# One-hots of a routing table in wide 16-bit VectorE operations, with a reordered drain of the routers

## The reference, cut to what matters

```
x = x + attention(layernorm(x), ctx, W_k, b_k, gamma, beta)      # x: 4 batches x 512 tokens x 512
x = x + moe(layernorm(x), Wg, W1, W2, W3)

def moe(x, Wg, W1, W2, W3):                                      # 8 experts, hidden size 352
    scores = einsum('btd,ed->bte', x, Wg)
    topk_s, topk_i = top_k(scores, 2)
    w = weights of the two chosen experts: softmax(topk_s), zero elsewhere
    for e in range(8):
        h = silu(x @ W1[e].T) * (x @ W2[e].T)
        y = y + w[..., e:e+1] * (h @ W3[e].T)
```

## Time and profile before

| | |
|---|---|
| time, median of 3 runs | 421.27 us (421.18 to 422.28) |
| time of the profiled execution | 422.17 us |
| its span in the profile | 420.1 us |
| TensorE busy | 366.2 us (87%) |
| VectorE busy | 273.6 us (65%) |
| ScalarE busy | 265.2 us (63%) |
| GpSimd busy | 187.0 us (45%) |
| mean granted TensorE clock | 0.907 of full speed |

### The profile page before, as it was taken

How to read it: one execution, slowest core, us unless ns; L and a number is a source line. 1 busy time by engine, 2 the same in 40 slices (tenths; PEclk the granted TensorE clock), 3 DMA queues, 4 the chain that set the end, 5 groups by cost and what they waited for, 6 DMA issues and landing times.

```text
span 420.1 us, 8336 instructions
## 1 busy us (share of the span) xinstructions
PE 366.2 (87%) x2321; PEld 244.9 (58%) x2321; DVE 273.6 (65%) x724; ACT 265.2 (63%) x457; POOL 187.0 (45%) x221
## 2 busy tenths in 40 slices
PE   6876997996948447799999999999999999999982
PEld 5543665765848234455566666666666666666650
DVE  0252565958668739999776676676676676676670
ACT  2287587855657619789666666666666666666660
POOL 2115364476896661355434434434434434434322
PEclk9998699599555569999999999999999999999997
DMA  7997889964741021224354354354354355354333
GB/s 233 418 420 275 273 290 370 355 230 160 243 166 37 26 75 28 50 52 70 83 103 75 78 102 77 75 103 75 78 102 78 75 102 80 75 100 79 77 48 51
DMA packets 21835, 57.62 MB, mean 137 GB/s; under 512 B 4832, under 2 KB 4960, under 8 KB 20256
## 3 DMA queue, kind: packets, MB, share of 16 engines
q0 software_dynamic: 8736, 20.53, 27.5%
q1 hardware_dynamic: 11040, 21.62, 14.6%
q10 hardware_dynamic: 2016, 14.94, 9.9%
HBM read 38.17 MB, written 18.91 MB: 136 GB/s over the span
## 4 chain that ended last, share of the span: by engine, by line
PE 52%; POOL 7%; DVE 7%; issue 6%; DMA 2%; ACT 2%; ACTq 1%; POOLq 1%; DVEq 0%
PE bank L1220 29%; PE bank L1254 15%; PE bank L1211 3%; POOL stage L429 3%; PE bank L1240 3%; DVE Wp L804 2%; DVE stage L951 1%; DMA out<-kvj_s,sidx 1%; POOL ng_s L469 1%; PE bank L1124 1%; POOL w3rs L476 1%; ACT stage L638 1%; DVE x_s L983 1%; POOL rstd L412 1%; DVE stage L767 1%
## 5 line engine op out<-in xcount | busy, mean ns | idle before, releaser
L951 DVE SCALAR_TENSOR_TENSOR stage<-W,w3sc,stage 128x512 f16<-128x512 f16 x117 | 84.2, 748 | 6.8 <-ACT stage L638 6.8
L1254 PE MATMUL bank<-stage,n_s 128*128 128x512 f16 (+1 forms) x351 | 82.2, 379 | 2.8 <-issue 1.5
L1220 PE MATMUL bank<-Wp,kvg_s 128*128 x480 | 79.9, 317 | 4.6 <-DVE kvg_s L957 4.6
L638 ACT ACTIVATE stage<-W,w3sc 128x512 f16 x117 | 80.2, 718 | 0.0
L1220 PE MATMUL bank<-Wp,kv_s 128*128 x456 | 74.3, 313 | 3.4 <-DVE kv_s L957 3.4
L484 POOL DMA_INDIRECT out<-oT_s,sidx x20 | 34.1, 1704 | 75.1 <-ACT oT_s L665 67.7
L1220 PEld LDWEIGHTS bank<-Wp,kvg_s 128*128 128x128 f16 x480 | 47.3, 99 | 31.5 <-issue 6.1
L484 POOL DMA_INDIRECT out<-kvj_s,sidx x19 | 32.4, 1706 | 66.2 <-ACT kvj_s L665 63.5
L1220 PEld LDWEIGHTS bank<-Wp,kv_s 128*128 128x128 f16 x456 | 44.4, 98 | 28.3 <-issue 4.8
L975 DVE TENSOR_TENSOR n_s<-bank,n_s 128x384 f16<-128x384 f32 x39 | 21.7, 557 | 54.9 <-ACT n_s L651 54.9
L1254 PEld LDWEIGHTS bank<-stage,n_s 128*128 128x128 f16 (+1 forms) x351 | 34.2, 98 | 36.1 <-issue 3.3
(11 more groups left out here) (184 smaller groups left out, 555.2 us busy)
## 6 DMA issues: line engine op xcount, KB each, us to landing
Wp<-in_w ACTq DMA_DIRECT2D x6, 1408.0 KB, 8.7
W<-in_w ACTq DMA_DIRECT2D x8, 768.0 KB, 5.3
stage<-in_xT SPq DMA_DIRECT2D x4, 1024.0 KB, 7.8
W<-in_x SPq DMA_DIRECT2D x12, 256.0 KB, 7.4
out<-W SPq DMA_DIRECT2D x12, 256.0 KB, 5.5
Wp<-in_w SPq DMA_DIRECT2D x2, 1408.0 KB, 12.9
n_table<-n_s SPq DMA_DIRECT2D x8, 256.0 KB, 3.2
n_table<-x_s SPq DMA_DIRECT2D x8, 256.0 KB, 3.0
```

Source lines behind the costliest of these rows:

```text
L638: eng.activation(w3p[t % 2][:, c * D:(c + 1) * D], W3[:, bass.ds(e * W3N + c * D, D)], ACT.Copy, scale=w3sc[:, bass.ds(e, 1)]).then_inc(s_ ...
L951: eng.scalar_tensor_tensor(w3p[r][:, W3N + c * D:W3N + (c + 1) * D], W3[:, bass.ds(e * W3N + c * D, D)], w3sc[:, bass.ds(e, 1)], w3p[r][:, ...
L1220: mm = eng.matmul(bank[2 * which + r][:, 0:H], n_, w_, start=(c == 0 and k == 0), stop=(c == DC - 1 and k == 2))
L1254: mm = eng.matmul(ybank(t - 1)[:, :], h_, w_, start=(c == 0 and k == 0), stop=(c == HC - 1 and k == 2))
```

## The change

The two one-hot matrices of a whole lot are made on VectorE by three instructions, all of whose operands are fp16: row one-hots, column one-hots, and a multiplication of the row one-hots by the token's number. For this, two tables are made once at the start: `steps8` (0 to 127, each number eight times) and `tok16`. The one-hots of a lot now lie interleaved, pair by pair innermost, so TensorE reads each with a step of eight elements. GpSimd makes no one-hots. TensorE's drain is reordered and has no `warm` matmuls. Lot 3 is placed ahead of the last group's router scores on VectorE. The zeros for the dump row are made in slot 17 and stored ahead of the last router weights. The split of expert 1's W1 and W2 on ScalarE goes behind the first `mT_evac`, and VectorE's first low half goes behind the list of experts.

```diff
-WARM_GATHER = 16
-WARM_DRAIN = 8
+WARM_GATHER = 12
...
-        qf = sb("qf", [P, G * TOPK])
-        rf = sb("rf", [P, G * TOPK])
+        qf = sb("qf", [P, G * TOPK], F16)
+        rf = sb("rf", [P, G * TOPK], F16)
+        steps8 = sb("steps8", [P, P, TPB * TOPK], F16)
+        tok16 = sb("tok16", [P, G, TOPK], F16)
...
@@ sync: the dump row's store
             batches(slot)
-            router_store(B - 1)
-
             eng.wait_ge(s_zr, 1)
             eng.dma_start(out[T:T + P, :], zrow[:, :]).then_inc(s_zst, 16)
+            router_store(B - 1)
...
@@ gpsimd: slot
-                if n in (11, 12):
-                    columns(0, 2 * n - 22, 2 * n - 20)
-                if n in (14, 15):
-                    columns(1, 2 * n - 28, 2 * n - 26)
-                if n == 18:
-                    columns(2, 0, 4)
+                if n == 17:
+                    eng.wait_ge(s_mp, B)
+                    eng.memset(zrow[:, :], 0.0).then_inc(s_zr, 1)
             gamma_keys(0)
             batches(slot)
-            columns(3, 0, 3)
-            columns(4, 0, 1)
-
-            eng.wait_ge(s_mp, B)
-            eng.memset(zrow[:, :], 0.0).then_inc(s_zr, 1)
...
@@ scalar: behind the slots
-            w12_high(1, 0)
             router_exp(B - 1)
-            w3_square(4)
-            w12_high(1, 1)
-            for k in range(5, E):
+            for k in range(4, E):
                 w3_square(k)
...
             mT_evac(0)
+            w12_high(1, 0)
+            w12_high(1, 1)
...
@@ vector
-            def columns(q, a, z):
-
-                g0 = GROUPS[q][0]
+            def columns(q):
+
+                g0, m = GROUPS[q]
+                i0, a = g0 % TPB * TOPK, g0 // TPB % 2
+                ring_free(eng, q)
+                cols, ring = slice(g0 * TOPK, (g0 + m) * TOPK), slice(i0, i0 + m * TOPK)
+                shape = [P, P, m * TOPK]
                 eng.wait_ge(s_rqf, 2 * q + 1)
-                ring_free(eng, q)
-                for c in range((g0 + a) * TOPK, (g0 + z) * TOPK):
-                    g, s = c // TOPK, c % RING
-                    eng.tensor_scalar(oh_r[:, s, :], iota[:, :], rf[:, c:c + 1], tok1[:, g:g + 1], ALU.is_equal, ALU.mult).then_inc(s_ohr, 1)
+                eng.tensor_tensor(oh_r[:, a, :, ring], steps8[:, :, ring], rf[:, None, cols].to_broadcast(shape), ALU.is_equal).then_inc(s_ohp, 1)
+                eng.wait_ge(s_rqf, 2 * q + 2)
+                eng.tensor_tensor(oh_c[:, a, :, ring], steps8[:, :, ring], qf[:, None, cols].to_broadcast(shape), ALU.is_equal).then_inc(s_ohc, 1)
+                eng.wait_ge(s_ohp, q + 1)
+                eng.tensor_tensor(oh_r[:, a, :, ring], oh_r[:, a, :, ring],
+                                  tok16[:, g0:g0 + m, :].rearrange("p g k -> p (g k)")[:, None, :].to_broadcast(shape), ALU.mult).then_inc(s_ohr, 1)
...
+                if n == 20:
+                    places(3)
+                    columns(3)
                 b3, i3 = lag(b, i, 4)
...
-                if i == 0 and real(b - 2):
+                if i == 0 and 1 < b < B:
                     places(b - 2)
-                if n in (11, 12):
-                    columns(0, 2 * n - 22, 2 * n - 20)
-                if n in (14, 15):
-                    columns(1, 2 * n - 28, 2 * n - 26)
                 if n == 18:
-                    columns(2, 0, 4)
-                    w12_low(0, 0)
+                    places(2)
+                if n in (11, 14, 18):
+                    columns((n - 11) // 3 if n < 18 else 2)
...
@@ tensor: drain
                 if n == 17:
                     router(B - 1, 0)
-                    rank(2)
                     turn_n(B - 1, 2)
                     router(B - 1, 1)
                 if n == 18:
+                    rank(2)
                     router(B - 1, 2)
-                    warm(ones16[:, :], WARM_DRAIN)
                     turn_n(B - 1, 3)
                 if n == 19:
-                    warm(ones16[:, :], WARM_DRAIN)
+                    table(1)
+                    rank(3)
                     router(B - 1, 3)
-                    table(2)
-                    rank(3)
                 if n == 20:
+                    table(2)
                     rank(4)
                     counts()
                     table(3)
```

More of the change, by code:

```diff
@@ L299, in ring_free @@
         def ring_free(eng, q):
+            eng.wait_ge(s_eoff, 3)
             eng.wait_ge(s_op, B)
@@ L903, in _ @@
             router_weights(B - 1)
-            places(last - 1)
             places(last)
-            columns(last - 1, 0, 3)
-            columns(last, 0, 1)
+            columns(last)
             eng.wait_ge(s_cntp, 1)
@@ L990, in _ @@
             eng.wait_ge(s_et, 1)
+            w12_low(0, 0)
             w12_low(0, 1)
@@ L1181, in slot @@
                     table(0)
-                if n == 16:
-                    table(1)
             eng.wait_ge(s_const, NCONST)
```

33 lines of the change are left out of this document (15 added, 18 removed).

## The result

The changed kernel takes 405.38 us (median of 4 runs, 404.62 to 407.42) against 421.54 us of the kernel before in the same job (421.18 to 422.28). The ratio is 0.9622, with a 95% interval of 0.9584 to 0.966: 16.2 us faster. I had forecast 410.0 us with a range of 406.5 to 416.2. The direction was right; the gain is 4.8 us larger than the sum, and the time lies outside the range. Two later jobs, each with one of the two kernels unchanged, gave 0.9618 and 1.0002 (experiments c2 and c1), so the gap is no accident of one job.

A forecast was written before the change was run, and what follows sets the result against it. Before the tiles, a chain of waits on GpSimd's column one-hots and the dump row's store was taken as the bound. Terms -7.2 + 0 - 3.1 - 1.1 + 0 = -11.4 us gave 410.0 us, range 406.5 to 416.2.

The forecast's parts named there:

- Step A: Slots 11 to 17, to the last normalised group, without GpSimd's column one-hots: -7.2 us.
- the term for the start of slot 11: In slot 11 VectorE has 1.9 us in place of 1.10, and 0.33 us of idle takes some: +0.5 us.
- Step B: From the last normalised group to the last places: again 11.8 us, so a change of 0.
- What is saved pays for columns 2 and 3: In the drain, dropping 16 warm matmuls and L804's 1.68 us offsets the column one-hots of two lots: 0.
- Step C: From the last places to `gidx`: 3.2 us in place of 6.3, as the table no longer awaits GpSimd: -3.1 us.
- rival 1: Wide instructions run at one element per cycle: +6.4 us, some 0.5 of it hidden, 416 us; chance 0.15.
- Rival 3: Wide instructions are slower than one element per cycle, over 1.6 us each; 426 us at the strided price; chance 0.04.
- Step D: From `gidx` to the first gather: 1.1 us in place of 2.24, no longer awaiting the dump row's store: -1.1 us.
- Step E: Start of the tiles: ScalarE's two w12_high fit into its wait for TensorE: 0.
- So it fits, with 0.6 us to spare: 0.: At the start of the tiles, ScalarE's added work takes 4.4 us where its next instruction started 5.0 us later.
- Rival 2: TensorE stays at 2.4 GHz through the drain: 408.3 us, 407 if the walk is pessimistic too; chance 0.11.
- 11 to 12 us from there to `w3rs` as before: Sign expected in the profile after: the time from the first gather to `w3rs` stays unchanged.

The follow-up runs named there:

- c2: The changed kernel timed once more with no edit: 404.72 us, 0.9618 of the kernel before.
- c1: The kernel before timed once more with no edit: 421.42 us, ratio 1.0002; its profiled execution took 421.50 us.
- e4: The changed kernel with the two constant tables `steps8` and `tok16` in fp32 instead of fp16: 411.76 us, 0.9791 of the kernel before.
- e5: The changed kernel with TensorE's old drain and the old places of lots 2 and 3 on VectorE: 407.52 us, 0.9679 of the kernel before.
- e7: The changed kernel with the splits of W1 and W2 of experts 0 and 1 back in their old places: 407.25 us, 0.9686 of the kernel before.
- e3: The kernel before with only the wide one-hots on VectorE; drain, zero store and splits as before: 408.88 us, 0.9687 of the kernel before.
- e1: The kernel before with only the dump row's zeros made in slot 17 and stored ahead of the last router weights: 417.54 us, 0.9907.
- e6: The changed kernel with one low half of expert 0's split put right behind the list of rows, beside the first gather: 407.11 us, 0.9672.
- e8: The changed kernel with 24 more warm matmuls in slots 15 and 16 and 12 more in slot 17: 404.79 us, 0.9617 of the kernel before.

## Why the prediction was wrong

The forecast beside two profiles, c1 for before (421.50 us) and the first of the changed kernel (405.16 us), both of executions near their medians. Each step is the time between the same two instructions in both (c1, then changed):

```
step                                       forecast   measured
A  up to the product of slot 11             +0.5      -0.6   (89.01 -> 88.37)
A  product to last xneg                     -6.0      -6.2   (30.80 -> 24.65)
A  xneg to last normalised group            -1.7      -1.7   (5.11 -> 3.44)
B  to the last places                        0        -0.8   (11.83 -> 11.06)
C  to gidx                                  -3.1      -3.0   (6.29 -> 3.28)
D  gidx to first gather                     -1.1      -1.7   (2.22 -> 0.51)
E  gather to the first copy (kvg_s)          0        -1.3   (6.27 -> 4.94)
E  copy to L629                              0        -0.4   (5.63 -> 5.28)
   the tiles, to the end                     0        -0.5   (262.24 -> 261.77)
sum                                        -11.4     -16.1
```

- *Step A* was right where it was worked out: the slots from the product of slot 11 to `xneg` and the normalisation behind it came within 0.2 us. What failed is the term for the start of slot 11. It took the 0.33 us of idle in the earlier trace rows for the room that slot has; c1 shows 2.47 us in the same code, and in e4, with 1.2 us an instruction, the product is no later (87.83). So no profile shows the 0.5 us. The other 0.6 us of this row are an earlier start of slot 11 than in c1, which is within the spread of profiles (87.02 to 90.72 us) and not shown to come from the change. The base itself was a late execution of that slot, with the last normalised group at 126.00 against 124.92 in c1.
- *Step B* was a walk that came out at no change; it was 0.8 us shorter. e5 and e7 show that both halves of the change matter there: with the old order it is 11.93 us, with the split back in slot 18 of the new order it is 12.56. With the old order the split cost nothing (11.92 in e3), so the 1.68 us counted as saved were not there as a term of their own. "What is saved pays for columns 2 and 3" was nearly right, with 0.8 us over.
- *Step C* was right: 3.28 us against 3.2. The wide instructions of the last pair, the count and the table's copy follow as walked. The price, on which rivals 1 and 3 hung, was right too (0.695 us against 0.69), and e4 shows rival 1's cost about as I had priced it (+6.4 forecast with 0.5 hidden; 7.1 to 7.3 by the medians, 4.9 in the profile). Rival 3 needs over 1.6 us an instruction; nothing of it is there.
- *Step D*: the store as a releaser went, as forecast, but I allowed 0.9 us from `gidx` to the gather, read from the landing of a store to the gather, and 0.2 for `gidx`; all of it takes 0.51 us from `gidx`'s start. The gain was put 0.6 us too low.
- *Step E is the step that failed*: "So it fits, with 0.6 us to spare: 0." It looked at ScalarE alone, and found rightly that its two high halves cost nothing (0.45 us to spare). It put at nothing what GpSimd pays beside VectorE there. In the kernel before, a split with two SBUF inputs started 0.25 us ahead of the first gather and another 0.17 us ahead of `w3rs`, and each held GpSimd up by 1.3 to 1.4 us:

```profile
146.11 1.69 DVE L804 SCALAR_TENSOR_TENSOR Wp<-Wp,wscale 128x1408 f16<-128x1408 f32 x1
...
153.97 1.68 DVE L804 SCALAR_TENSOR_TENSOR Wp<-Wp,wscale 128x1408 f16<-128x1408 f32 x1
154.14 3.05 POOL L476 TENSOR_TENSOR w3rs<-w3sum,half 128x8 f32<-128x8 f32 x1 [2.71 <-DVE w3sum L936]
```

  The two go for different reasons. The split at the gather starts 2.0 us behind `gidx` before and after; it is the gather that now leaves ahead of it, by step D's own 1.7 us. e1 shows it with no split moved, e3 too, and e6 takes it back: 1.3 us. At `w3rs` the split is what moved: it waits for ScalarE's high half, which the change put later, and comes second; where that is undone (e7, e3), the time from the copy to L629 is 5.62 and 5.61 us instead of 5.28: 0.3 us. Together 1.7 us of the miss. The row of 2.58 us was in front of me, and so was the pattern: 1.15 us beside a VectorE instruction and 0.77 alone. I even wrote that the two engines get in each other's way, applied it to slot 14, where it could only cost, and not to the place where the change takes it away.
- *Rival 2* (TensorE stays at 2.4 GHz, 408.3 us): not what happened. The clock from 118 to 131 us is 0.50, the lower level, as before. The reason for the surplus lies elsewhere. Where e8 does hold the clock up to 118 us, step B is 1.2 us shorter in the profile, close to the 1.1 that this rival was priced at, but the median does not move.
- *The range* failed because four terms (slot 11, B, D, E) were all put too low and fell the same way: 1.1 + 0.8 + 0.6 + 1.7 us, and 0.5 in the tiles, of which I can't say that it is more than the spread of profiles (261.75 to 262.37 us over the runs, the kernel before with 261.80). Its lower end, 406.5, was 3.5 us below the forecast and made of rival 2 and errors of the walk.
- *One sign was misnamed*: "11 to 12 us from there to `w3rs` as before". From the first gather to `w3rs` it was 154.14 - 146.36 = 7.8 us before and is 6.4 now; the 11.9 us are those to ScalarE's first activation of a tile, 10.2 now. Both shrank, by the 1.3 to 1.7 us that step E lacks.

What stays open: whether e6 loses more than the 1.14 us at the gather, what gave the 0.6 us ahead of slot 11 and the 0.5 in the tiles, and why e8's gain in step B is not seen in its median.

## What to carry to other kernels

When an instruction with two SBUF inputs is moved on VectorE, or a GpSimd instruction beside it, look at what GpSimd launches beside which, at the old place and at the new: a gather or a tiny root on the path can be longer by the rest of that instruction, and a duration well above that of its neighbours (2.58 us against 0.95 for the next two gathers) is the sign of it. An engine that is the bound of a stage by latency, as GpSimd was here, is worth emptying even at narrow prices: two thirds of the gain came without the wide instructions (3.5 us of it from the store and the gather, which moving the store alone gives too). Edits that gain alone need not add up: e5 and e7 cost 2.6 and 2.9 us, both together no more. And do not take the idle time in front of one instruction of one profile for the room of that place; a second profile of the same kernel moved it from 0.33 to 2.47 us.

## What the runs showed of the hardware

- **A GpSimd instruction that is launched while a two-input VectorE instruction runs takes longer by about what is left of that instruction.** A first gather launched 0.23 to 0.39 us behind the start of the split takes 2.40 to 2.60 us, launched first 1.24 to 1.27. What was left and what was lost: 1.51 and 1.38 us (`w3rs`, c1), 1.46 and 1.35 (gather, c1), 1.29 and 1.15 (gather, e6), 0.80 and 0.67 (third gather, e6), 0.51 and 0.38 (`x_s` of the earlier trace rows), 0.39 and 0.27 (third gather, changed kernel; 0.95 us alone). The loss is 0.11 to 0.14 us less than the rest each time.

```profile
133.87 1.69 DVE L794 SCALAR_TENSOR_TENSOR Wp<-Wp,wscale 128x1408 f16<-128x1408 f32 x1
134.76 1.62 POOL L454 DMA_INDIRECT ng_s<-n_table,gidx  x1 [0.30 <-issue]
```

```profile
97.87 0.68 DVE L819 CUSTOM_DVE_ANT_0 L_s<-L_s,beta_s 128x512 f32<-128x512 f32 x1
```

- **There is an exception at the very start.** The second gather of the changed kernel, 0.03 us behind a split's start (132.86 and 132.83), takes 0.96 us, as without one; so does that of e1 (0.04 us behind, 0.95 us). What decides between 0.03 and 0.23 us, no run here shows.
- **Matmuls that read 16-bit operands with a step of eight elements take 0.25 us each, at either level of the clock.** A table of eight takes 2.06 us at a granted clock of 0.50 (120.00 us) and 2.02 us at 97.26 us, where the granted clock is 1.00 (96 to 100 us). In the kernel before, eight matmuls with contiguous operands took 1.01 us at 0.50. So a table costs the 1 us more that I had allowed. In the drain it is hidden: from 117.25 us to the last places VectorE is never idle for more than 0.27 us.

```profile
120.00 2.06 PE L1043 MATMUL bank<-stage 128*128 128x128 f16 x8
```

- **The first part of the kernel drifts from one execution to the next.** The product of slot 11 starts between 87.0 and 90.7 us over fourteen profiles with nearly the same code up to there. The granted clock of 60 to 80 us differs too, 0.82, 1.00 and 0.83 in the profiles of before, c1 and c2, but these have the product at 90.72, 89.01 and 88.32 us, so that clock alone does not order them. A difference of a microsecond between two profiles in the slots says nothing without a second profile of each.
